# Field sums moved from TensorE to VectorE: scaling in place on ScalarE, a running sum of quads on VectorE, TensorE once a block

## What is computed

```python
gathered = jax.vmap(lambda table, idx: table[idx], in_axes=(0, 1), out_axes=1)(emb, xi)
e = gathered * xv[:, :, None]
s = jnp.sum(e, axis=1)
qi = 0.5 * (s * s - jnp.sum(e * e, axis=1))
h = jax.nn.relu(xv @ W1 + b1)
x = jnp.concatenate([qi, h], axis=1)
return x @ W2 + b2
```

## Time and profile before

| | us |
|---|---|
| median of 3 runs | 739.86 (739.0 to 741.13) |
| profiled execution, its own time | 740.26 |
| its span, first to last instruction | 738.5 |

### The profile page before, as it was taken

How to read it: one execution, slowest core, us unless ns; L and a number is a source line. 1 busy time by engine, 2 the same in 40 slices (tenths; PEclk the granted TensorE clock), 3 DMA queues, 4 the chain that set the end, 5 groups by cost and what they waited for, 6 DMA issues and landing times.

```text
span 738.5 us, 3855 instructions
## 1 busy us (share of the span) xinstructions
PE 324.3 (44%) x1094; PEld 49.0 (7%) x1094; DVE 329.8 (45%) x389; ACT 329.7 (45%) x529; POOL 485.7 (66%) x524
## 2 busy tenths in 40 slices
PE   1535345363443544345353453534535344344433
PEld 0001000010000000001010000100000000000000
DVE  3432644506455054641536415364253642526438
ACT  2444545354353553544534534344343544435444
POOL 6757667576675757757657577575775757757663
PEclk9999999955555555555555555555555555555555
DMA  7757757576675756757757567575675757757664
GB/s 226 201 141 206 201 149 204 141 206 182 165 205 144 204 165 183 203 141 202 204 139 204 157 185 201 143 203 151 194 196 147 204 143 201 202 141 203 169 174 123
DMA packets 33687, 132.00 MB, mean 179 GB/s; under 512 B 8641, under 2 KB 8769, under 8 KB 33634
## 3 DMA queue, kind: packets, MB, share of 16 engines
q0 software_dynamic: 32768, 130.06, 64.1%
q1 hardware_dynamic: 800, 1.31, 0.6%
q10 hardware_dynamic: 98, 0.40, 0.2%
HBM read 131.72 MB, written 0.01 MB: 178 GB/s over the span
## 4 chain that ended last, share of the span: by engine, by line
POOL 53%; issue 23%; DMA 8%; another core or an unknown queue 7%; ACT 4%; DVE 3%; PE 2%; POOLq 0%; DVEq 0%
POOL gathered L159 53%; DMA gathered<-emb,index_rows 8%; ACT squares L173 4%; DVE squares L295 2%; PE sum_ps L218 2%; DMA index_raw<-index 0%; DVE weighted L281 0%; DVE weighted_hidden L333 0%; POOLq L155 0%; PE y_ps L237 0%; DVE sum_lines L288 0%; DVE y L368 0%; DVE hidden_lines L288 0%; DVE index_wrap L262 0%
## 5 line engine op out<-in xcount | busy, mean ns | idle before, releaser
L159 POOL DMA_INDIRECT gathered<-emb,index_rows x512 | 484.1, 946 | 242.2 <-issue 143.2
L173 ACT ACTIVATE squares<-gathered,values 128x496 f32<-128x496 f32 x512 | 320.8, 697 | 392.1 <-DMA gathered<-emb,index_rows 392.0
L295 DVE SCALAR_TENSOR_TENSOR squares<-squares,w_ps 128x1984 f32<-128x1984 f32 (+2 forms) x136 | 277.3, 2096 | 400.5 <-issue 279.3
L218 PE MATMUL sum_ps<-gathered,weights 128*32 128x496 f32 x1024 | 265.5, 1032 | 409.5 <-DMA gathered<-emb,index_rows 407.1
L218 PEld LDWEIGHTS sum_ps<-gathered,weights 128*32 128x32 f32 x1024 | 30.0, 140 | 639.9 <-DMA gathered<-emb,index_rows 504.9
L230 PE MATMUL hidden_ps<-w_b,value_rows 33*128 33x512 f32 x64 | 59.2, 1069 | 1.2 <-issue 1.2
L230 PEld LDWEIGHTS hidden_ps<-w_b,value_rows 33*128 33x128 f32 x64 | 18.1, 311 | 44.0 <-issue 44.0
L272 DVE SCALAR_TENSOR_TENSOR weights<-y_ps,values 128x1024 f32<-128x1024 f32 x16 | 19.5, 1220 | 0.0
L333 DVE SCALAR_TENSOR_TENSOR weighted_hidden<-hidden_ps,w_all 128x1024 f32<-128x1024 f32 x16 | 19.5, 1220 | 0.0
L295 DVE DVE_READ_ACCUMULATOR squares<-squares,w_ps 128x1 f32 x136 | 11.2, 82 | 0.0
L281 DVE SCALAR_TENSOR_TENSOR weighted<-sum_squared,w_ps 128x496 f32<-128x496 f32 x16 | 10.7, 666 | 0.0
(11 more groups left out here) (20 smaller groups left out, 5.1 us busy)
## 6 DMA issues: line engine op xcount, KB each, us to landing
gathered<-emb,index_rows POOLq DMA_INDIRECT x512
w_all<-w SPq DMA_DIRECT2D x1, 760.0 KB
values<-value SPq DMA_DIRECT2D x1, 256.0 KB, 2.9
value_rows<-value_t ACTq DMA_DIRECT2D x1, 256.0 KB
index_raw<-index SPq DMA_DIRECT2D x1, 240.0 KB, 4.9
w_b<-w ACTq DMA_DIRECT2D x1, 128.0 KB
index_raw<-index SPq DMA_DIRECT2D x1, 16.0 KB, 2.5
w_b<-b ACTq DMA_DIRECT2D x1, 4.0 KB
```

Source lines behind the costliest of these rows:

```text
L159: nc.gpsimd.indirect_dma_start(out=gathered[:, n % slots, j, :], out_offset=None, in_=emb, in_offset=bass.IndirectOffsetOnAxis(ap=index_ro ...
L173: return nc.scalar.activation(squares[:, s // deep, j, s % deep], gathered[:, n % slots, j], ACT.Square, scale=values[:, g:g + 1])
L218: last = nc.tensor.matmul(sum_ps[j * COLS:(j + 1) * COLS, i % 2, 0:dim], weights[:, i % 2, s * GROUPS + j, :], gathered[:, n % slots, j, : ...
L295: return nc.vector.scalar_tensor_tensor(of, of, -0.5, w2_ps[:, 0:dim].unsqueeze(1).to_broadcast([P, quads_of.stop - quads_of.start, dim]), ...
```

## The change

The scaling is taken apart from the squaring. ScalarE multiplies each landed group by its value in place in `gathered` (`scale`, four instructions a quad), and squares two whole quads, eight groups, with one instruction (`square`). VectorE adds the scaled quads of a block with one instruction a quad (`add`) into `running_ps` in PSUM; the first add of a block (s = 1) reads quads 0 and 1, both from `gathered`, and the last (s = 7) writes `added_up`. TensorE then sums over the four fields of a partition once a block, four matmuls (`sum_fields`) in place of 32. The weight matrices and their refill go. `gathered` has 8 slots for 5, and GpSimd waits for `squared` (of pairs now) and `added` in place of `squared` and `summed`. VectorE's eight weighing instructions of a half block are spread between the adds of the next. In the last block the squares of three quads are summed by TensorE (`late_squares`) and weighed once. Long runs of removed lines are left out below; they stand in the listing above.

```diff
-    slots = 5
+    slots = 8
...
-        weights = sb("weights", [P, 2, in_block, COLS])
         gathered = sb("gathered", [P, slots, GROUPS, dim])
-        squares = sb("squares", [P, 2, GROUPS, deep, dim])
+        squares = sb("squares", [P, 2, deep, GROUPS, dim])
+        added_up = sb("added_up", [P, 2, GROUPS, dim])
         weighted = sb("weighted", [P, dim])
-        weights_sum = sb("weights_sum", [P, blocks])
+        weighted_late = sb("weighted_late", [P, dim])
...
-        sum_ps = psum("sum_ps", [P, 2, 512])
+        sum_ps = psum("sum_ps", [P, 512])
+        running_ps = psum("running_ps", [P, GROUPS, 512])
         hidden_ps = psum("hidden_ps", [P, halves, 512])
-        y_ps = psum("y_ps", [P, 512])
...
-                        pool.wait_ge(squared, n - slots + 1)
-                        pool.wait_ge(summed, n - slots + 1)
+                        i_of, s_of = divmod(n - slots, quads)
+                        pool.wait_ge(squared, (n - slots) // 2 + 1)
+                        pool.wait_ge(added, i_of * adds + max(s_of, 1))
...
-            def square(n, j):
+            def scale(n, j):
                 i, s = n // quads, n % quads
                 g = i * in_block + s * GROUPS + j
-                return nc.scalar.activation(squares[:, s // deep, j, s % deep],
-                                            gathered[:, n % slots, j], ACT.Square,
-                                            scale=values[:, g:g + 1])
+                rows_of_one = gathered[:, n % slots, j]
+                return nc.scalar.mul(rows_of_one, rows_of_one, values[:, g:g + 1])
+            def square(n, count, groups):
+                s = n % quads
+                kept = slice(s % deep, s % deep + count)
+                held = slice(n % slots, n % slots + count)
+                return nc.scalar.activation(squares[:, s // deep, kept, groups],
+                                            gathered[:, held, groups], ACT.Square)
             def square_sums(i):
-                act.wait_ge(summed, (i + 1) * quads)
+                act.wait_ge(summed, i + 1)
                 if i > 0:
                     act.wait_ge(sum_squared_used, i)
-                nc.scalar.activation(sum_squared[:], sum_ps[:, i % 2, 0:dim],
+                nc.scalar.activation(sum_squared[:], sum_ps[:, 0:dim],
                                      ACT.Square).then_inc(sum_squared_ready, 1)
             act.wait_ge(values_loaded, 16)
             for n in range(all_quads - 1):
                 i, s = n // quads, n % quads
-                if s % deep == 0 and i > 0:
-                    act.wait_ge(normed, (i - 1) * 2 + s // deep + 1)
                 act.wait_ge(fetched[n % slots], (n // slots + 1) * 16 * GROUPS)
                 for j in range(GROUPS):
-                    last = square(n, j)
-                last.then_inc(squared, 1)
+                    last = scale(n, j)
+                last.then_inc(scaled, 1)
+                if n % 2 == 0 and n > 0:
+                    if (n - 2) % deep == 0 and n - 2 >= quads:
+                        act.wait_ge(normed, (n - 2) // deep - 1)
+                    act.wait_ge(scaled, n)
+                    square(n - 2, 2, slice(0, GROUPS)).then_inc(squared, 1)
                 if s == 3 and i > 0:
                     square_sums(i - 1)
-            for j in range(GROUPS):
-                if j % pairs == 0:
-                    act.wait_ge(last_fetched[j // pairs], 16 * pairs)
-                square(all_quads - 1, j).then_inc(last_squared, 1)
+            act.wait_ge(scaled, all_quads - 1)
+            square(all_quads - 2, 1, slice(0, GROUPS)).then_inc(squared, 1)
+            for half in range(pairs):
+                act.wait_ge(last_fetched[half], 16 * pairs)
+                of = slice(half * pairs, (half + 1) * pairs)
+                for j in range(of.start, of.stop):
+                    scale(all_quads - 1, j).then_inc(last_scaled, 1)
+                act.wait_ge(last_scaled, of.stop)
+                square(all_quads - 1, 1, of).then_inc(last_squared, 1)
             square_sums(blocks - 1)
...
+            def sum_fields(i, j):
+                return nc.tensor.matmul(sum_ps[j * COLS:(j + 1) * COLS, 0:dim], own_sample[:],
+                                        added_up[:, i % 2, j, :], start=True, stop=True,
+                                        tile_position=(0, j * COLS))
+            def late_squares(n):
+                s = n % quads
+                for j in range(GROUPS):
+                    last = nc.tensor.matmul(hidden_ps[j * COLS:(j + 1) * COLS, 0, 0:dim], own_sample[:],
+                                            squares[:, s // deep, s % deep, j], start=(s == deep),
+                                            stop=(s == quads - 2), tile_position=(0, j * COLS))
+                last.then_inc(late_summed, 1)
             pe.wait_ge(w1_loaded, 48)
+            pe.wait_ge(ones_ready, 1)
+            pe.wait_ge(own_sample_ready, 1)
             for i in range(blocks):
...
+                if i > 0:
+                    pe.wait_ge(hidden_used, i)
+                for h in range(halves):
+                    last = nc.tensor.matmul(hidden_ps[:, h, :], value_rows[:, i * P:(i + 1) * P],
+                                            w1_b1[:, h * 512:(h + 1) * 512], start=True, stop=True)
+                last.then_inc(hidden_ready, 1)
+                if i + 1 < blocks:
+                    if i > 0:
+                        pe.wait_ge(sum_squared_ready, i)
+                    pe.wait_ge(added, (i + 1) * adds)
                     for j in range(GROUPS):
...
+                        last = sum_fields(i, j)
                     last.then_inc(summed, 1)
...
+            pe.wait_ge(hidden_used, blocks)
+            for n in range(all_quads - deep, all_quads - 1):
+                pe.wait_ge(squared, n // 2 + 1)
+                late_squares(n)
+            pe.wait_ge(sum_squared_ready, blocks - 1)
+            for j in range(GROUPS):
+                pe.wait_ge(added, blocks * adds - 1 + j + 1)
+                last = sum_fields(blocks - 1, j)
+            last.then_inc(summed, 1)
...
+            def add(n, groups):
+                i, s = n // quads, n % quads
+                sums = running_ps[:, groups, 0:dim]
+                return nc.vector.scalar_tensor_tensor(
+                    added_up[:, i % 2, groups] if s == quads - 1 else sums,
+                    gathered[:, n % slots, groups], 1.0,
+                    gathered[:, n % slots - 1, groups] if s == 1 else sums,
+                    ALU.mult, ALU.add)
+            def may_add(n):
+                i, s = n // quads, n % quads
+                if n > 1:
+                    dve.wait_ge(added, i * adds + s - 1)
+                if s == quads - 1 and i > 1:
+                    dve.wait_ge(summed, i - 1)
+            def add_quad(n):
+                if n % quads > 0:
+                    dve.wait_ge(scaled, n + 1)
+                    may_add(n)
+                    add(n, slice(0, GROUPS)).then_inc(added, 1)
...
             for i in range(blocks):
...
+                for half in range(2):
+                    first = i * quads + half * deep
+                    i_of, half_of = (i, 0) if half else (i - 1, 1)
+                    for t in range(deep if i + 1 < blocks or half == 0 else deep - 1):
+                        add_quad(first + t)
+                        if first > 0:
+                            if t == 0:
+                                dve.wait_ge(squared, first // 2)
+                            last = weigh_squares(i_of, half_of, t, slice(0, deep),
+                                                 norms[:, i_of, half_of, t:t + 1])
+                            if t == deep - 1:
+                                last.then_inc(normed, 1)
+                        if half == 0 and t == 0:
+                            dve.wait_ge(hidden_ready, i + 1)
+                            nc.vector.scalar_tensor_tensor(
+                                weighted_hidden[:], hidden_ps[:], 0.0,
+                                w2_all[:, dim:].rearrange("p (h c) -> p h c", h=halves),
+                                ALU.max, ALU.mult, accum_out=hidden_part[:, i:i + 1]
+                                ).then_inc(hidden_used, 1)
+                        if half == 1 and t == 0 and i > 0:
+                            weigh_sums(i - 1)
+            weigh_squares(blocks - 1, 0, deep - 1, slice(0, deep), norms[:, blocks - 1, 0, deep - 1:deep]
+                          ).then_inc(normed, 1)
...
-            dve.wait_ge(normed, 2 * end)
+            dve.wait_ge(normed, 2 * end + 1)
             nc.vector.tensor_tensor(norm_lines[:, 0:end], norms[:, 0:end, 0], norms[:, 0:end, 1], ALU.add)
...
+            n = all_quads - 1
+            may_add(n)
+            for half in range(pairs):
+                of = slice(half * pairs, (half + 1) * pairs)
+                for j in range(of.start, of.stop):
```

(20 more changed lines are left out.)

86 lines of the change are left out of this document (15 added, 71 removed).

## The result

The changed kernel takes 752.84 us (median of 4 runs, 749.99 to 753.14) beside 739.72 us for the kernel before on the same chip: 1.0166 times as long, 95% interval 1.0138 to 1.0195. Forecast was 664.7, range 655 to 694, with 0.10 for slower. The forecast was wrong in sign, and the time lies outside the range.

The account below looks back on a forecast made before the run. POOL's gathers bound the kernel, 639.9 us at their own pace plus 84.8 of stalls from TensorE's late counts. 738.5 - 84.8 + 8.4 + 1.2 = 663.3 us of span, 664.7 as time; range 655 to 694.

Parts of the forecast that it names:

- With TensorE out of the wait the stalls go: -84.8: POOL's wait before gathers: TensorE's late counts cause all 84.8 us of stalls, which go when `added` replaces `summed`.
- the tail: Behind the last gather: ACT and VectorE have more left to do, 17.9 us against 9.5, so +8.4.
- the first term: POOL's wait: the stalls go, -84.8 us, last gather done at 644.2.
- ACT is ruled out: Cause of POOL's stalls: not ScalarE, whose recorded instruction ends show it had left the slot at 403.5.
- rival B: POOL's stalls were not TensorE's count, perhaps a gather queue limit; all 84.8 us stay, 748 us, slower; chance 0.07.
- The first adds: VectorE's first add of each block, both operands in SBUF, lengthens gathers: 16 x 0.075 = 1.2 us, dearest 32.
- rival A: First adds hold the gathers that start within them: 16 x 1.4 = 22.4 us, giving 686, up to 696; chance 0.22.
- the cheap end: First adds: a gather meeting one is only 0.075 us longer, 16 times, 1.2 us in all.
- The sizes: Single instructions on ScalarE and VectorE: pair's square 3.85 us (2.5 to 4.8), add 2.15, scaling 0.60 back to back.
- rival C's loads: ScalarE reloads its table at each change between scaling and squaring, 1.28 us each: 790 us and more; chance 0.03.
- its mild form: Unseen waits between ACT and VectorE add a few us a block: 680 to 720 us; chance 0.11 together with rival D.
- rival D: TensorE's lateness moves to ACT's square of the sums: 665 to 690 us; chance 0.11 together with C's mild form.

Follow-up runs that it names:

- the cut kernel: The changed kernel with ScalarE's scaling cut to 8 of 496 columns: 682.5 us where the kernel before takes 655, 751.9 us on a 735 chip.
- first_psum_again: Repeat on a 735 chip of the changed kernel with each block's first add reading its second operand from PSUM: 752.3 us, 1.026 of the kernel before.
- after_again: The changed kernel run again without edits on a 735 chip: 751.8 us, 1.025 of the kernel before.

## Why the prediction was wrong

**The step that failed** is the first of the change: "With TensorE out of the wait the stalls go: -84.8". The 84.8 us were real, and it was TensorE's count that POOL stood for: in 19 of the 20 gaps over 1 us an update of `summed` is on record 0.01 to 0.03 us before POOL's wait passes. But they were not the price of having TensorE in the wait. With TensorE out of it, 50.8 us of stalls stay in the changed kernel, and the held gathers and the tail take more than the rest. On the 735 chips the pace stays at 1.38 to 1.42 us a gather with 5 or 8 slots, with full or tiny matmuls, squares and scalings, with whole or half rows, and whether POOL waits for TensorE and ScalarE or for ScalarE and VectorE. The wait that names itself last is only where the lateness shows. On the 655 chips the kernel before has no stall, and its 655.2 us is just what the first term made of 739.9. I took the engine that released POOL, 0.06 us after it had gone on itself, for the cause. The same rows held the warning: TensorE went on inside a quad, with 0.73 us of idle time put down to "issue". An engine that itself stands still with nothing to wait for is held too; it is not shown to be the source.

Two readings on the way to that step were weak. "ACT is ruled out: its instruction ends are recorded" doesn't follow: ScalarE's count came 8 us after its recorded end in the profile after. And the "unknown queue" of the chain, which spoke for rival B, is no sign of a queue, since most updates are missing from that trace.

**Rival B** (the stalls stay, the longer end decides, 748, chance 0.07) came nearest: 752.8. Its mechanism, a limit of the gather queue, isn't shown: rows land just as promptly between stalls as on a chip without them, and 128 gathers went at 1.26 us. What it had right is that the stalls don't go with TensorE. Its number is in part luck: the stalls did not all stay (84.9 fell to 50.8), the held gathers took 23.2 of that back, and the tail grew by 22.5 where it had 8.4. The gathers ended 9.7 us earlier, which by its own point (8.4) would have come out about even; the tail decided.

**The tail** was forecast at +8.4 and is +22.5. The mechanism (more work behind the last landing) is right: the cut kernel on a 655 chip has +5.8. The same cut kernel on a 735 chip has a tail of 30.8 for 15.2, so some 16 us go with the chip; that they are the late counts is likely and not shown apart. In the first profile VectorE is through with its full-size steps 21.6 us after the last gather (740.9), on the 655 chip after 5.3 (668.45). I take it that with 8 slots POOL runs further ahead of VectorE, so that what is late in the gathers is paid behind them; no run tests it.

**The first adds** (rival A, 0.22, 16 x 1.4 = 22.4 us) happened nearly to the number: 23.2 us in 16 gathers. Taking the cheap end of 1.2 was wrong: the 1.02 us gather of the earlier trace rows had only 0.2 us of the other instruction left, and could tell neither reading from the other. Here that costs no time, as first_psum_again shows beside after_again (752.3 and 751.8); on a 655 chip long gathers are 19.0 us. The Trainium skill (SBUF — State Buffer, section Who interferes with whom) has a VectorE instruction with two SBUF inputs contend with a GpSimd instruction that reads SBUF, the loser blocked for the whole of the other instruction; the 2.90 us gather, begun 0.15 us into the add and held past its end, agrees. The same section, which is about the ports of SBUF, has it that TensorE and ScalarE never wait on anyone there; the matmuls 2.8 us apart, with operands ready, are held by something, and no run here shows whether it is a port.

**The sizes** were good. The pair's square took 3.51 us (3.85 forecast, bounds 2.5 and 4.8), an add 2.23 (2.15), a scaling 0.70, with one table load (rival C's loads fell, and with ScalarE's work cut by a third nothing changed, so its mild form too). ScalarE's square of the sums waited 7.6 us for TensorE in all, and that at the very end (rival D fell). The Trainium skill (ScalarE: Activation LUTs, section What ACT_TABLE_LOAD costs) has two fixed costs: the 280 ns that the prediction took are for an instruction whose bias is a pointer operand and give 3.59 us; with immediate scale and bias it is 186 ns, which gives 3.49, nearer to the 3.51 measured.

**On the 655 chips** the uncut changed kernel wasn't run. With its scaling cut it takes 682.5, and I see nothing by which the whole scaling could make it quicker, so I take it to be at least 4% slower there. By the same terms, with a base without stalls, the working of the prediction would give 653.9 + 8.4 + 22.4 = 684.7 of span, 678.3 measured for the cut kernel.

**Open** is what holds TensorE's and ScalarE's instructions and counts on the 735 chips, why in steps of 0.70 us, and whether its pace goes by gathers, by their rows or by the instructions that the consumers retire. It goes neither by bytes, nor by TensorE's clock, nor by how long those instructions are. One rival was not tested: the recording itself. Every time here has a span and a granted clock beside it, so none was taken without some recording; on just the chips that stall most updates are missing from the trace, and their number goes by the gathers, 16 each, which bytes and the consumers' work leave as it is. A time without any recording, on both kinds of chip, would tell. No version beat the kernel before on either kind of chip with its computation whole.

## What to carry to other kernels

Before a stall is booked as a gain, ask whether its length follows from the engine blamed for it: make that engine's work small and see whether the stall goes, and look whether that engine also stands still with nothing to wait for. Compare the mean pace and where the stalls begin, not the single gaps: the ring of 8 slots only dealt the same 84.9 us out anew. Count the semaphore updates in a trace before trusting the names of its releasers. And know the chip: here two chips of one sort differed by 12% on the same kernel, more than any edit, and a change judged on one of them is judged for that one; though as far as it was measured this change costs time on both. An add with both operands in SBUF beside a stream of indirect gathers holds the gather that starts within it to 0.81 us past its end, which costs time where the gathers are the bound.
